# Rotary attention: causal mask out of TensorE's products, selection on GpSimd, addition inside VectorE's maximum, scores two groups ahead

## What is computed

```python
Q = _rope(split_heads(x @ wq.T), THETA)      # x: layer-normed, 16 heads of 8 channels
K = _rope(split_heads(x @ wk.T), THETA)
V = split_heads(x @ wv.T)
scores = jnp.einsum('bhqd,bhkd->bhqk', Q, K) / math.sqrt(8)
causal_mask = jnp.triu(jnp.ones((N, N), dtype=bool), k=1)
scores = jnp.where(causal_mask, -jnp.inf, scores)
attn = jax.nn.softmax(scores, axis=-1)
out = jnp.einsum('bhqk,bhkd->bhqd', attn, V)
return out.transpose(0, 2, 1, 3).reshape(B, N, D) @ wo.T
```

## Time and profile before

| | us |
|---|---|
| median of 3 runs | 2896.11 |
| lowest and highest | 2887.38, 2908.32 |
| the profiled execution, its own time | 2902.76 |
| its span, first to last instruction | 2900.9 |

### The profile page before, as it was taken

How to read it: one execution, slowest core, us unless ns; L and a number is a source line. 1 busy time by engine, 2 the same in 40 slices (tenths; PEclk the granted TensorE clock), 3 DMA queues, 4 the chain that set the end, 5 groups by cost and what they waited for, 6 DMA issues and landing times.

```text
span 2900.9 us, 44112 instructions
## 1 busy us (share of the span) xinstructions
PE 1753.3 (60%) x13716; PEld 1146.8 (40%) x13716; DVE 1334.2 (46%) x3558; ACT 970.8 (33%) x1719; POOL 1057.4 (36%) x1177
## 2 busy tenths in 40 slices
PE   3765506776666454556776676422325488888975
PEld 2544404555444242244554454100124234455443
DVE  3648811222334677473222333543215466666644
ACT  3651102232223321312232222356761123444342
POOL 2001777724651774757714651771000200000000
PEclk9985557778878655557788787655555568998985
DMA  8941118999997111117999997120000000000001
GB/s 234 382 181 29 51 53 275 325 304 292 321 289 241 52 52 54 52 55 244 327 308 294 310 301 241 51 54 8 4 2 0 0 1 1 1 1 2 1 1 29
DMA packets 332506, 393.39 MB, mean 136 GB/s; under 512 B 57952, under 2 KB 222512, under 8 KB 332208
## 3 DMA queue, kind: packets, MB, share of 16 engines
q1 hardware_dynamic: 215616, 171.43, 19.0%
q10 hardware_dynamic: 83984, 153.13, 15.4%
q0 software_dynamic: 32768, 67.17, 7.7%
HBM read 242.13 MB, written 164.63 MB: 140 GB/s over the span
## 4 chain that ended last, share of the span: by engine, by line
PE 36%; DVE 15%; DMA 13%; ACT 11%; issue 10%; SPq 9%; POOL 6%; DVEq 0%; ACTq 0%; POOLq 0%
DMA arena<-expert_blocks 12%; SPq L1819 6%; ACT arena L955 5%; PE psum L1918 4%; PE psum L1909 4%; POOL slot_rows L1725 4%; PE psum L448 3%; SPq L1815 3%; PE psum L1347 2%; PE psum L1900 2%; PE psum L1328 2%; PE psum L432 2%; PE psum L993 1%; PE psum L427 1%; ACT arena L1210 1%
## 5 line engine op out<-in xcount | busy, mean ns | idle before, releaser
L1736 POOL DMA_INDIRECT arena<-slot_results,SLOTS x512 | 490.7, 958 | 503.1 <-DMA slot_results<-arena 285.8
L1725 POOL DMA_INDIRECT slot_rows<-arena,SLOTS x512 | 493.4, 964 | 309.4 <-issue 308.8
L1699 DVE COPY arena<-psum 128x512 f32<-128x512 f32 x288 | 198.6, 690 | 742.3 <-PE psum L1918 719.4
L1909 PE MATMUL psum<-arena 128*64 128x128 f32 x2304 | 236.5, 336 | 278.4 <-DMA arena<-expert_blocks 271.0
L1779 ACT ACTIVATE arena<-psum 128x512 f32<-128x512 f32 x288 | 171.9, 597 | 476.4 <-PE psum L1900 467.6
L1909 PEld LDWEIGHTS psum<-arena 128*64 128x64 f32 x2304 | 154.5, 165 | 349.0 <-issue 291.5
L169 POOL TENSOR_SCALAR rstd<-mv 128x4 f32<-128x4 f32 x32 | 6.2, 193 | 772.3 <-DVE mv L577 771.8
L1900 PE MATMUL psum<-ident,arena 128*128 128x128 f32 x1152 | 231.6, 335 | 84.9 <-DMA arena<-slot_rows 84.3
L1918 PE MATMUL psum<-arena 64*128 64x128 f32 x2304 | 253.3, 350 | 0.0
L1786 ACT ACTIVATE arena<-psum 128x256 f32<-128x256 f32 x288 | 110.4, 383 | 338.5 <-PE psum L1909 335.3
L1918 PEld LDWEIGHTS psum<-arena 64*128 64x128 f32 x2304 | 189.6, 230 | 64.4 <-issue 64.2
(11 more groups left out here) (234 smaller groups left out, 3064.5 us busy)
## 6 DMA issues: line engine op xcount, KB each, us to landing
arena<-expert_blocks SPq DMA_DIRECT2D x1152, 96.0 KB
arena<-slot_rows ACTq DMA_DIRECT2D x288, 256.0 KB
slot_results<-arena ACTq DMA_DIRECT2D x288, 256.0 KB
slot_rows<-zeros SPq DMA_DIRECT2D x2, 18432.0 KB, 84.2
slot_rows<-arena,SLOTS POOLq DMA_INDIRECT x512, 2.2
arena<-slot_results,SLOTS POOLq DMA_INDIRECT x512
expert_blocks<-in_expert_w SPq DMA_DIRECT2D x1, 7680.0 KB, 26.0
expert_blocks<-in_expert_w SPq DMA_DIRECT2D x1, 5120.0 KB, 52.7
```

What stands on the lines that cost most here:

```text
L1699: dve.tensor_copy(YSB[:, p].rearrange("p (c h) d -> p h c d", h=2), psum[:, first:first + 2, 0:256].rearrange("p h (c d) -> p h c d", c=2) ...
L1725: pool.indirect_dma_start(out=slot_rows[h], out_offset=bass.IndirectOffsetOnAxis(ap=SLOTS[:, t, k:k + 1], axis=0), in_=XNH[:, t], in_offse ...
L1736: pool.indirect_dma_start(out=GATHERED[:, t % TPI, k], out_offset=None, in_=slot_results[h], in_offset=bass.IndirectOffsetOnAxis(ap=SLOTS[ ...
L1909: mm = pe.matmul(psum[lo:lo + INTER, 2 + 5 * (p % 2), o:o + P], EWB[:, p, q, 0:INTER], XSBT[:, p, P * q:P * q + P], start=True, stop=True, ...
```

## The change

Four things, all in the rotary layer.

- The mask products L1347 and L432 go. In the pass for the maximum VectorE's two reductions become two `tensor_tensor_reduce`, which add a mask in SBUF (`LATER`, zeros and then `mask_qk`, bfloat16) to the scores and take the maximum in one instruction, with a written by-product `MASKED`. The maximum is no longer negated there, so `largest_rows` gets one more instruction, a product with -1 of 64 elements, and a wait for it.
- In the pass for the weights nothing is masked in the scores. The exponential is written with the blocks of 128 queries outermost, the diagonal blocks in front of the third (`diagonal_first` writes PSUM in that order), and GpSimd sets the 1,024 elements a partition of the two diagonal blocks of a group to zero above the diagonal with `affine_select`, in place (`causal`).
- `PR2` has four buffers for two. TensorE's order is now scores g+2, then values g; values g wait for GpSimd's selection. The 32 heads of the maxima stand among scores 1 to 4 and values 0 to 3 as before; scores 1 and 2 of a step have no value products between them. ScalarE's exponentials each stand one place further ahead of its copies.
- The mask for VectorE is made by GpSimd behind the three memsets, and VectorE waits for it at the layer's start.

```diff
+        def diagonal_first(pe, bank, kt, qt, k):
+            v = psum[:, bank, 0:384].rearrange("p (b q) -> p b q", q=P)
+            pe.matmul(v[:, 0:3:2, :], kt[0:k, 0:128], qt[0:k, :].rearrange("k (b q) -> k b q", q=P), start=True, stop=True, skip_group_check=True)
+            return pe.matmul(v[:, 1, :], kt[0:k, 128:256], qt[0:k, 128:256], start=True, stop=True, skip_group_check=True)
...
-        PR2 = view([P, 2, 4, 384])
+        PARTS = 4
+        PR2 = view([P, PARTS, 3, 4, P])
+        LATER = view([P, 2 * P], BF16)
+        MASKED = view([P, 2, 3 * P], BF16)
...
         def rope_vector(dve, layer):
             r = front_run(layer)
+            dve.wait_ge(r_zero, 5)
...
-                    dve.tensor_reduce(MX[:, 2 * b, h:h + 1], psum[:, bank, 0:128], AX.X, ALU.max, negate=True).then_inc(r_max.sem, 1)
-                    dve.tensor_reduce(MX[:, 2 * b + 1, h:h + 1], psum[:, bank, 128:384], AX.X, ALU.max, negate=True).then_inc(r_max.sem, 1)
+                    dve.tensor_tensor_reduce(MASKED[:, m % 2, 0:P], psum[:, bank, 0:128], LATER[:, P:], 1.0, NEG, ALU.add, ALU.max, MX[:, 2 * b, h:h + 1]).then_inc(r_max.sem, 1)
+                    dve.tensor_tensor_reduce(MASKED[:, m % 2, P:], psum[:, bank, 128:384], LATER, 1.0, NEG, ALU.add, ALU.max, MX[:, 2 * b + 1, h:h + 1]).then_inc(r_max.sem, 1)
...
-                dve.tensor_copy(QS2[:, :, MROW], m).then_inc(r_mrows.sem, 1)
+                dve.tensor_scalar(ML, MX.rearrange("p t h -> p (t h)"), -1.0, None, ALU.mult).then_inc(r_minus.sem, 1)
+                dve.wait_ge(r_minus.sem, r_minus.at(0, s))
+                dve.tensor_copy(QS2[:, :, MROW], ML).then_inc(r_mrows.sem, 1)
...
             def weigh(i, g):
                 act.wait_ge(r_sc.sem, r_sc.at(0, i, g + 1))
-                act.wait_ge(r_av.sem, r_av.at(0, i, g - 1))
-                act.activation(PR2[:, g % 2], psum[:, 4:8, 0:384], ACT.Exp, scale=DH ** -0.5).then_inc(r_exp.sem, 1)
+                act.wait_ge(r_av.sem, r_av.at(0, i, g - PARTS + 1))
+                act.activation(PR2[:, g % PARTS].rearrange("p b r q -> p r b q"), psum[:, 4:8, 0:384].rearrange("p r (b q) -> p r b q", q=P), ACT.Exp, scale=DH ** -0.5).then_inc(r_exp.sem, 1)
...
+            pool.memset(LATER[:, 0:P], 0.0).then_inc(r_zero, 1)
+            pool.tensor_copy(LATER[:, P:], mask_qk[:]).then_inc(r_zero, 1)
...
+            def causal(i):
+                for g in range(8):
+                    pool.wait_ge(r_exp.sem, r_exp.at(0, i, g + 1))
+                    stand(pool)
+                    diagonal = PR2[:, g % PARTS, 0:2].rearrange("p b r q -> p (b r) q")
+                    pool.affine_select(diagonal, diagonal, [[0, 8], [1, P]], ALU.is_ge, 0.0, base=0,
+                                       channel_multiplier=-1).then_inc(r_sel.sem, 1)
...
                 for u in range(2):
+                    causal(i2 * 2 + u)
                     norm(i2 * 2 + u + 3)
                     values(i2 * 2 + u + 2, u)
...
-                    pe.matmul(psum[:, bank, 0:128], q[0:SPLIT, 0:128], kk[0:SPLIT, 0:128], start=True, stop=False, skip_group_check=True)
-                    pe.matmul(psum[:, bank, 128:384], q[0:SPLIT, 128:256], kk[0:SPLIT, :], start=False, stop=False, skip_group_check=True)
-                    v = psum[:, bank, 0:384].rearrange("p (a q) -> p a q", q=P)[:, 0:3:2, :]
-                    pe.matmul(v, identb[:], mask_qk[:].unsqueeze(1).broadcast_to([P, 2, P]), start=False, stop=True, skip_group_check=True).then_inc(r_s1.sem, 1)
+                    pe.matmul(psum[:, bank, 0:128], q[0:SPLIT, 0:128], kk[0:SPLIT, 0:128], start=True, stop=True, skip_group_check=True)
+                    pe.matmul(psum[:, bank, 128:384], q[0:SPLIT, 128:256], kk[0:SPLIT, :], start=True, stop=True, skip_group_check=True).then_inc(r_s1.sem, 1)
...
                 for rr in range(4):
-                    head_scores(pe, 4 + rr, head(KT2, u, b, head_of(n, rr)), head(QT2, u, b, head_of(n, rr)), SCORE_K)
+                    mm = diagonal_first(pe, 4 + rr, head(KT2, u, b, head_of(n, rr)), head(QT2, u, b, head_of(n, rr)), SCORE_K)
+                    if rr == 3:
+                        mm.then_inc(r_sc.sem, 1)
                     if between is not None:
                         between()
-                for rr in range(4):
-                    mm = mask_scores(pe, 4 + rr)
-                mm.then_inc(r_sc.sem, 1)
...
-                pe.wait_ge(r_exp.sem, r_exp.at(0, i, g + 1))
+                pe.wait_ge(r_sel.sem, r_sel.at(0, i, g + 1))
...
                 scores(i, u, 0)
+                some = one if left >= 1 else None
+                scores(i, u, 1, some)
                 for g in range(8):
                     between = one if g < 4 and left >= 1 else None
-                    if g < 7:
-                        scores(i, u, g + 1, between)
+                    if g < 6:
+                        scores(i, u, g + 2, some if g < 3 else None)
```

More of the change, by code:

```diff
@@ L449, in weigh_values @@
                                        ones4[:, head_of(n, r) % 4, :] if half else vp(kt, head_of(n, r)),
-                                       pr[:, r, 0:256] if kt == 0 else pr[:, r, 256:384],
+                                       pr(kt, r),
                                        start=(n == half == kt == 0), stop=(n == 3 and half == kt == 1),
@@ L499, in values @@
                     pe.wait_ge(a_ot.sem, a_ot.before(0, i))
-                weigh_values(pe, n, lambda kt, h: VP[:, u, 2 * (h // 8) + kt, h % 8, :], PR[:, n % 2]).then_inc(a_av.sem, 1)
+                weigh_values(pe, n, lambda kt, h: VP[:, u, 2 * (h // 8) + kt, h % 8, :],
+                             lambda kt, r: PR[:, n % 2, r, 256 * kt:384 if kt else 256]).then_inc(a_av.sem, 1)
             def output(i):
@@ L1054, in program @@
         r_max = signal("r_max", 4 * NH)
+        r_minus = signal("r_minus")
         r_mrows = signal("r_mrows", 5)
@@ L1057, in program @@
         r_exp = signal("r_exp", 8, start=START + 8)
+        r_sel = signal("r_sel", 8)
         r_av = signal("r_av", 8, start=START + 8)
@@ L1214, in step @@
                 weigh(i, 1)
+                weigh(i, 2)
                 if left >= 2:
                     tokens(i + 2)
-                weigh(i, 2)
+                weigh(i, 3)
                 if left >= 2:
                     projected(i + 2, 0)
-                weigh(i, 3)
+                weigh(i, 4)
                 if left >= 2:
                     projected(i + 2, 1)
-                weigh(i, 4)
+                weigh(i, 5)
                 if left >= 2:
@@ L1226, in step @@
                     projected(i + 2, 3)
-                weigh(i, 5)
                 weigh(i, 6)
+                weigh(i, 7)
                 if left >= 1:
@@ L1231, in step @@
                     transposed(i + 1, 1 - u, 9)
-                weigh(i, 7)
                 if left >= 1:
@@ L1265, in rope_gpsimd @@
             pool.memset(KS2, 0.0).then_inc(r_zero, 1)
-            pool.wait_ge(r_zero, 3)
+            pool.memset(LATER[:, 0:P], 0.0).then_inc(r_zero, 1)
+            pool.tensor_copy(LATER[:, P:], mask_qk[:]).then_inc(r_zero, 1)
+            pool.wait_ge(r_zero, 5)
             pool.memset(KS2[:, :, MROW:MROW + 3], 1.0).then_inc(r_zero, 1)
-            pool.wait_ge(r_zero, 4)
+            pool.wait_ge(r_zero, 6)
             def norm(s):
@@ L1288, in rope_gpsimd @@
                 for u in range(2):
+                    causal(i2 * 2 + u)
                     norm(i2 * 2 + u + 3)
                     values(i2 * 2 + u + 2, u)
+            causal(STEPS - 4)
             norm(STEPS - 1)
             values(STEPS - 2, 0)
+            causal(STEPS - 3)
             values(STEPS - 1, 1)
+            causal(STEPS - 2)
+            causal(STEPS - 1)
         def rope_tensor(pe, layer):
             r = front_run(layer)
-            pe.wait_ge(r_zero, 4)
+            pe.wait_ge(r_zero, 6)
             def project(s, j):
@@ L1369, in values @@
                     pe.wait_ge(r_ot.sem, r_ot.at(0, i, b))
-                weigh_values(pe, n, lambda kt, h: VP2[:, u, 2 * b + kt, h, :], PR2[:, g % 2], between).then_inc(r_av.sem, 1)
+                weigh_values(pe, n, lambda kt, h: VP2[:, u, 2 * b + kt, h, :],
+                             lambda kt, r: PR2[:, g % PARTS, 1, r, :] if kt else PR2[:, g % PARTS, 0:3:2, r, :], between).then_inc(r_av.sem, 1)
             def output(i):
```

3 lines of the change are left out of this document (1 added, 2 removed).

## The result

| | before | after |
|---|---|---|
| median, us | 2893.5 (8 runs, 2886.95 to 2908.32) | 2926.26 (8 runs, 2914.28 to 2932.31) |
| the profiled execution, its span, us | 2902.76, 2900.9 | 2925.83, 2924.1 |
| granted clock over the span | 0.723 | 0.682 |
| from L1263's first memset to the layer's last exponential, us | 509.4 | 540.7 |
| a steady step, start to start of the maxima, us | 58.0 to 58.3 | 64.5 to 65.0 |

The account below looks back on a forecast made before the run. TensorE was taken to bound each step's first part, VectorE and ScalarE the second. Six steps gain 34 us, the seventh 8, the last 2, the front 3: 47 in all, median 2896.1 to 2849, range 2818 to 2885.

Parts of the forecast that it names:

- the first part after the change: Stretch of a step with the 32 row maxima: forecast 25.4 us against 31.7, 6.3 us a step gained.
- A + 6.8: Forecast end of the output products, in us after A, the moment VectorE is free for the maxima.
- rival A: TensorE's clock returns late, 2876, chance 0.14; or stays at 1.2 GHz throughout, 2931, chance 0.07.
- The low-clock rival: TensorE's clock stays at 1.2 GHz throughout: seven steps lose 38 us, 35 us slower, 2931; chance 0.07.
- A + 34.4: Forecast end of the maxima at 1.2 GHz, counted from VectorE being free for them; 2.7 us later than now.
- the front: 32 heads ahead of the steps: 4.2 us gained, 1.5 lost to VectorE waiting for GpSimd memsets: 3.
- every steady step recovered: Argument against a clock low throughout: TensorE's clock came back in each steady step of the kernel before.
- split end 13.8 after the maxima: VectorE's last subtraction for the rotated rows: 11.5 us, plus 0.3 sign change, plus 2.0 beside selections.
- pair 0.66 with a ceiling of 1.05: VectorE's two new maximum operations for a head: 0.66 us taken, floor 0.53, ceiling 1.05.
- selection 1.5: GpSimd's selection of 1,024 elements a partition, eight a step: 1.5 us each, covered in the first part.
- Rivals B and C: B: maximum takes two cycles an element, 2923, chance 0.06. C: long selection, 2865 (0.06) or 3010 (0.03).
- The sharing: VectorE slowed by two selections while building rotated rows: 2.0 us a step, bounds 1.2 and 3.0.

Follow-up runs that it names:

- e4: Changed kernel with both kinds of mask products put back on TensorE; lead, selection and masked maximum stay: 1.0099 of before.
- e11: Changed kernel plus 6, 13 and 4 unread dense products a step, each on 48 of the array's 128 rows: 1.0083 of before.
- e12: Changed kernel plus 6, 13 and 4 unread dense products a step, on all 128 rows and 32 of 128 columns: 0.9916 of before.
- e3_max: Kernel before with the masked maximum alone (L1347 gone); scores' mask products stay, no lead, no selection: 0.9977 of before.
- e9: Changed kernel plus 6, 13 and 4 unread 128x128 identity products where TensorE waits at a step's start: 0.9916 of before.
- e7: Kernel before with the masked maximum and 6 and 8 unread dense identity products at a step's start: 0.9868 of before.
- e6: Kernel before with 12 and 10 unread dense identity products at a step's start, nothing else changed: 0.9970 of before.
- e1: Kernel before with only the lead: TensorE two score groups ahead, four exponential buffers, exponentials one place earlier on ScalarE: 1.0054 of before.
- e2: Changed kernel with the maxima as before (mask product L1347 and plain reductions); lead, selection and mask-free scores stay: 1.0092 of before.
- e5: Changed kernel plus 12, 28 and 8 unread dense identity products where TensorE waits at a step's start: 1.0037 of before.

## Why the prediction was wrong

- **The step that failed** is "the first part after the change", where the groups are priced at full clock behind the output products (A + 6.8): 25.4 us, measured 36.6 at 0.50. Behind it stands the sentence in rival A, "in steady steps it came back about 7 us after A, behind the dense output products". It came back there with mask products around the output (e4: with them 0.86, without them 0.50); with only the products of 48 and 51 rows and the value products of 32 columns around them, the same output products (L1403) brought it back in none of the five steady steps. That it is the 128 rows of the mask products that do it is carried over from e11 and e12, and not shown for the masks themselves. The text even says that "what stands around those is thinner", and gives a clock that stays low 0.07.
- **The low-clock rival is what happened**, but its 2931 for 2926.26 is partly luck. Its first part, A + 34.4, is added up wrong: laid out like the forecast's, its own prices (5.1; output 3.4; value groups 7.2 - 2.6 = 4.6; transposes 0.8; projections 1.5; last scores 0.8) give A + 36.7, and 36.6 was measured. For the rest of a step it had 2.7 us more, measured 1.6 to 2.0. It charged 5.4 us to each of seven steps: the five steady ones lost 6.8, the seventh 3.1, and the first, at low clock before as well, gained 2.9; the last step gained 1.4, which it left out, and the front gained 1.5 for 3 (90.3 to 88.8 us from the memset to the first exponential). It also set 10.15 us a group against 7.15, though only the second holds a projection (L1308, 0.75 us).
- **Its argument against, "every steady step recovered", was the mistake.** That a state returns in six steps of one program says nothing of how near it was to not returning. e3_max, which lacks one product a head, has both kinds of steps.
- **The arithmetic at full clock was nearly right.** Forecast first part 25.4, e9 24.3 to 25.2 (with VectorE's pair at the measured 0.56 for 0.66 the forecast would be about 24); steps of 52 to 53, e9 51.4 to 54.7 in the four that kept the clock, from first exponential to first exponential; split end 13.8 after the maxima, measured 13.8; transposes 16.9, measured 16.9; pair 0.66 with a ceiling of 1.05, measured 0.56; selection 1.5, measured 1.09, and 1.44 beside VectorE. Still, e9's layer gained 27.4 us on before's and not 47: its first step and one steady step were at 0.62 and 0.66.
- **Rivals B and C fell** with these last two numbers.
- **The sharing** was put at 2.0 us and is 2.0 (13.8 less 11.5 less the sign change's 0.3), by two errors that cancel: the selections are shorter than 1.5 us, and VectorE lost nine tenths of their 2 x 1.09 us and not two thirds. The second pair of L1099 (L1086 before) took 1.65 us for 0.76 beside a selection, L1101 of the changed kernel (L1088 before) 2.14 us beside the next. By the Trainium skill's rule ("SBUF — State Buffer", Who interferes with whom), a GpSimd instruction and a VectorE one with two SBUF inputs exclude each other for the whole instruction, and one with a single SBUF input is free outside VectorE's two-port modes; the selections of 1.44 and 1.09 us would cost up to 2.5 us. The trace agrees in part, with 0.89 us for the pair of products and 0.92 for L1101 against the 1.22 us that the same operation took before; the first selection itself took 0.35 us longer than the others.
- **Not foreseen:** a selection also meets the normed tokens, L597 (L590 before), which took 1.99 us in place of 1.21 in before's same step. That is ahead of A, which the prediction held unchanged, and costs each steady step 0.8 us. The prediction took every operation with a single SBUF input to be free of GpSimd and left out the exception; L597 reads one SBUF tensor, and one of its four instructions took 1.11 us for 0.34. Whether it ran in a two-port mode the trace does not show.
- **The balance of a step**: 4.9 in the first part, 0.7 to the transposes, 0.8 in L597, together 6.4 of the 6.6 to 7 us by which a steady step grew; the rest is not placed. From first exponential to first exponential five steady steps grew by 34.1 us and the seventh by 3.1; the first shrank by 2.9 (it was at low clock before too), the last by 1.4, the front by 1.5: the layer's 31.3.
- **Which part of the change is worth what**, by the layer's length: of e7's 43.7 us the dense products alone are 11.2 (e6), and the masked maximum with the clock up is the other 32.5. The lead costs 17.5 us alone (e1). Selection, mask-free scores and lead together bring nothing that e7 lacks: where both keep the clock, its steps take 51.1 us against some 53 in e9. (The layers, 465.7 and 482.0 us, lie further apart, since e9's first step and one steady step ran at low clock.)
- **Still open:** why single steps of e2, e3, e5, e7, e9 and e12 lose the clock that their neighbours keep, and why the value products, on all 128 rows, don't bring it back in after. The rows of the array are shown to matter for products added in one place, and no further. Whether the lead helps if the selections are kept away from VectorE's rotation was not tried.

## What to carry to other kernels

Before removing products from an engine whose clock varies, read the granted clock in windows of a few us around the place where it rises, and ask which instructions it rises behind; if those are the ones to go, price the stretch at half clock as a forecast and not as a remote rival. An engine that is busy all the time is no evidence that it runs fast. Where a wait ahead of thin products costs the clock, a few products on all 128 rows in it can buy it back in most steps, if they fit into the wait (e9 against e5).

## What the hardware showed

- TensorE stayed at 0.50 for 36.6 us while busy 34.0 of them. The Trainium skill ("TensorE: Matmul & The Clock Gate", Part 1) says that the throttled clock is the default and that activity releases it. By that rule, if busy time is the activity, the first part should have recovered early; the trace disagrees, for products mostly of 48 and 51 rows and of 128 rows on 32 columns.
- Added products on 48 rows in place of 128, of equal duration (0.27 us), left the clock low in three of five steady steps (0.50, 0.55) and late in the other two (0.82, 0.83); 32 columns in place of 128 changed nothing (1.00 in four of five).
- A `tensor_tensor_reduce` on PSUM against a bfloat16 mask takes as long as a plain reduction (0.42 us for 256 elements, 0.41 before), plus a read of the accumulator of 0.08 us which mostly overlaps: 0.03 us more a pair.
- A selection of 1,024 float32 elements a partition takes 1.09 us.
- One selection can hold a VectorE operation that reads a single SBUF tensor: four of 128 elements (L597) took 1.99 us for 1.21.
